# Constant matmuls in TensorE's waits around a selective scan and at the ends of attention, and an earlier load of the first expert weights

## What is computed

```
x = x + 0.5 * ffn(ln(x))     # gated, four 512-wide layers, ternary weights
x = x + mamba(ln(x))         # in_proj, conv of 4, x_proj, softplus, scan, out_proj
x = x + 0.5 * ffn(ln(x))     # the same weights again
x = x + 0.5 * moe(ln(x))     # 64 experts of 88, top 8 in 4 of 8 groups, 2 shared
x = x + attention(ln(x))     # 8 query heads, one key/value head, causal, 512 tokens
x = x + 0.5 * moe(ln(x))     # the same weights again
```

## Time and profile before

| | |
|---|---|
| median of three runs | 1762.87 us |
| the profiled execution | 1760.58 us, of which span 1758.8 us |
| TensorE busy | 1605.8 us (91%) |
| VectorE busy | 1272.3 us (72%) |
| ScalarE busy | 1016.4 us (58%) |
| GpSimd busy | 992.7 us (56%) |
| mean granted TensorE clock | 0.974 of 2.4 GHz |

### The profile page before, as it was taken

How to read it: one execution, slowest core, us unless ns; L and a number is a source line. 1 busy time by engine, 2 the same in 40 slices (tenths; PEclk the granted TensorE clock), 3 DMA queues, 4 the chain that set the end, 5 groups by cost and what they waited for, 6 DMA issues and landing times.

```text
span 1758.8 us, 24391 instructions
## 1 busy us (share of the span) xinstructions
PE 1605.8 (91%) x6936; PEld 1196.0 (68%) x6936; DVE 1272.3 (72%) x2156; ACT 1016.4 (58%) x2065; POOL 992.7 (56%) x955
## 2 busy tenths in 40 slices
PE   7997667877799989999899899998998999999998
PEld 5775323333367767777688677886886778878887
DVE  5555699999855756788578567885775678856665
ACT  4343655454434446676477666664776666656665
POOL 1101067766510028888433378894333888978887
PEclk9999789999999999999999999999999999999999
DMA  2000000000000036666300056663000566656674
GB/s 104 10 1 1 0 1 1 0 0 0 8 0 1 1 88 165 163 166 165 85 1 1 6 143 154 170 174 86 1 1 5 146 152 174 172 141 172 172 173 107
DMA packets 57678, 136.75 MB, mean 78 GB/s; under 512 B 10251, under 2 KB 33251, under 8 KB 57187
## 3 DMA queue, kind: packets, MB, share of 16 engines
q1 hardware_dynamic: 57571, 135.47, 30.0%
HBM read 133.33 MB, written 2.10 MB: 77 GB/s over the span
## 4 chain that ended last, share of the span: by engine, by line
PE 64%; DVE 4%; ACT 3%; issue 2%; POOL 2%; POOLq 0%; PEldq 0%; PEld 0%; DMA 0%; SPq 0%; DVEq 0%; ACTq 0%
PE ps L226 18%; PE ps L227 18%; PE ps L228 17%; PE ps L1488 2%; PE ps L1473 1%; PE ps L1474 1%; PE ps L1475 1%; PE ps L774 1%; POOL m_hc L984 1%; POOL e_lo L234 1%; PE ps L366 1%; PE ps L1476 0%; DVE p L1661 0%; PE ps L377 0%; PE ps L254 0%
## 5 line engine op out<-in xcount | busy, mean ns | idle before, releaser
L234 POOL TENSOR_TENSOR e_lo<-e_h,e_hi 128x512 fp32r<-128x512 f32 (+1 forms) x368 | 476.4, 1295 | 131.1 <-ACT e_hi L231 120.7
L1140 ACT ACTIVATE e_s<-ps 128x512 f32<-128x512 f32 (+1 forms) x368 | 220.4, 599 | 271.5 <-PE ps L228 270.8
L1296 DVE TENSOR_TENSOR ps<-e_s,ps 128x512 f32<-128x512 f32 x352 | 244.7, 695 | 179.3 <-PE ps L228 145.1
L226 PE MATMUL ps<-xn_hi,eh 128*128 128x512 f32 x704 | 284.8, 405 | 10.3 <-ACT e_s L1140 7.4
L227 PE MATMUL ps<-xn_lo,eh 128*128 128x512 f32 x704 | 279.5, 397 | 0.0
L228 PE MATMUL ps<-xn_hi,el 128*128 128x512 f32 x704 | 278.8, 396 | 0.0
L1301 DVE TENSOR_TENSOR e_h<-ps,rwb 128x512 f32<-128x512 f32 x352 | 243.3, 691 | 16.2 <-DVE ps L1296 4.8
L984 POOL TENSOR_TENSOR m_hc<-m_h,m_c 128x512 f32<-128x512 f32 x128 | 172.5, 1348 | 125.3 <-DVE m_h L940 122.9
L234 POOL TENSOR_TENSOR el<-e_raw,eh 128x128 fp32r<-128x128 f32 (+1 forms) x352 | 221.8, 630 | 26.7 <-ACT eh L1129 26.7
L231 ACT ACTIVATE e_hi<-e_h 128x512 fp32r<-128x512 f32 (+1 forms) x368 | 229.3, 623 | 7.4 <-DVE e_h L1301 7.3
L774 PE MATMUL ps<-m_hc,const 128*128 128x512 f32 x256 | 149.5, 667 | 48.8 <-POOL m_hc L984 43.9
(11 more groups left out here) (232 smaller groups left out, 3293.5 us busy)
## 6 DMA issues: line engine op xcount, KB each, us to landing
e_raw<-in_experts SPq DMA_DIRECT2D x176, 192.0 KB, 3.9
rwb<-rw_rows SPq DMA_DIRECT2D x64, 352.0 KB
rwb<-rw_rows SPq DMA_DIRECT2D x80, 256.0 KB
rwb<-rw_rows SPq DMA_DIRECT2D x32, 320.0 KB
rwb<-rw_rows SPq DMA_DIRECT2D x48, 192.0 KB
rwb<-rw_rows SPq DMA_DIRECT2D x32, 224.0 KB
rwb<-rw_rows SPq DMA_DIRECT2D x32, 160.0 KB
rwb<-rw_rows SPq DMA_DIRECT2D x80, 64.0 KB
```

Of the source, the lines that this page charges most:

```text
L226: pe.matmul(out, w_hi, x_hi, start=start, stop=False, skip_group_check=True)
L234: return eng.tensor_tensor(lo, full, hi.bitcast(F32), ALU.subtract)
L1140: act.activation(e_s[0:rows_, buf, :], ps[0:rows_, 4, :], ACT.Silu).then_inc(S["silu"], 1)
L1296: dve.tensor_tensor(ps[:, bank, :], e_s[:, buf, :], ps[:, 5, :], ALU.mult).then_inc(S["gated"], 1)
```

## The change

Nine calls of `spin` are added to TensorE's list: 20 before the loop of the projections, 8 at the top of each of its three turns, 18 before the last `x_proj`, 8 after it, 12 ahead of the wait of the last output projection of the mixer, 6 at the end of the mixer; and, at the end of each of the two attention phases, 10 before the last `out_proj` and 6 after it. Counted as they run, that is 20 + 24 + 18 + 8 + 12 + 6 + 2 x 16 = 120 constant matmuls. On SyncE's queue the store of the routing rows moves behind the first four loads of `e_raw`.

```diff
             one_spread(pe, L, LAST)
+            spin(pe, 6, 20)
             pe.wait_ge(*M("dt_w", 2))
             pe.wait_ge(*L("xn_lo", NB))
             with pe.Fori(0, NB - 1) as i:
+                spin(pe, 6, 8)
                 in_proj(i + 1, bass.ds((i + 1) * T, T))
                 x_proj(i)
+            spin(pe, 6, 18)
             x_proj(NB - 1)
+            spin(pe, 6, 8)
...
             def finish(i, blk, q):
                 if q == 4:
+                    if isinstance(i, int):
+                        spin(pe, 0, 12)
                     after(pe, "x_new", i)
...
             for ch in range(SLOTS):
                 moe_weights(sp, S, ch)
+            if not before:
+                moe_store_rows(sp, R, half)
             sp.wait_ge(*R(f"rw_out{half}", 16))
...
                 if not last:
                     q_proj(i + 1, cut(i + 1), 1)
                     score(i + 1, 0)
+                else:
+                    spin(pe, 0, 10)
                 out_proj(i, HEADS - 1)
+                if last:
+                    spin(pe, 0, 6)
...
             moe_load_small(sp, R1)
-            moe_store_rows(sp, R1, 0)
             moe_load_first(sp, E1A, 0, R1, None)
...
             mix_pe(pe, LN[1])
+            spin(pe, 0, 6)
             end_phase(pe)
```

## The result

The changed kernel takes 1748.4 us (median of four runs, 1746.81 to 1750.39), with 1762.5 us for the kernel before on the same chip: a ratio of 0.9923, 95% interval 0.9905 to 0.9942, so 14.1 us are gone. Measured once more, on another chip, it took 1747.9 us (five runs), with 1762.8 for the kernel before: ratio 0.9915 (0.9901 to 0.9928), 15.0 us less. The prediction was 1747, range 1741 to 1756. Both intervals lie more than the 0.3% away from no change that the prediction named as the bound of what can be told.

What follows compares the result with a forecast made beforehand. TensorE, mostly busy at full clock, was taken to lose time where waits let its clock fall. Terms -4.2 - 3.7 - 5.4 - 1.5 - 0.45 = -15.3 us gave 1745.3, or 1747.6 on the median; 1747 was taken, range 1741 to 1756.

Steps and rivals of the forecast that it cites:

- Projections: Projections of phase 1: spins fill TensorE's waits and hold the clock, -4.2 us, bounds -2 and -5.
- The gap of 2 us: Projections, before in_proj(1): 2.0 us left empty by the spins; if the clock falls there, only -2 us is gained.
- the signs that the prediction named: Profile after: clock 1.00 from 168 to 209, `bc` at 205.5 instead of 209.78, the scan's first product 4 us sooner.
- Mixer's end and layernorm: End of mixer and layernorm of phase 2: +0.3 hold-up, -4.0 from full clock, -3.7 us; bounds -2 and -5.7.
- Phase 3: Start of phase 3: earlier `e_raw` load saves 3.7 us of wait, full clock another 1.7; -5.4 us, bounds -3.7 and -6.
- First attention's end: First attention's end and phase 5's first tiles: -1.6 from full clock, +0.1 hold-up; -1.5 us, bounds -0.7 and -2.2.
- Second: Second attention's end: +0.75 as spins delay the next phase, -1.2 on its tiles; -0.45 us, bounds +0.7 and -1.2.
- C: Whole kernel: spins do not hold the clock, only the earlier load's gain remains; -3.6 us, 1759; chance 0.05.
- D: Ends of mixer and attention, last x_proj: spins at 0.42 to 0.45 us outlast their waits; +12 us, 1775; chance 0.03.
- B: Whole kernel: the clock holds at some places only; -9.4 us, 1753.5; chance 0.18.
- A: Four low-clock stretches: removed low time gives half of itself everywhere, 18 us, with the load 21.7; 1741; chance 0.06.

Runs made afterwards that it cites:

- spins_only: The changed kernel with the store of the routing rows put back ahead of the first expert-weight loads, all 120 spins kept: 1755.0 us, ratio 0.9949.
- the doubled kernel: The changed kernel with 36, 24 and 20 spins where it has 18, 12 and 10, so that they outlast their waits: 1756.1 us, ratio 0.9956.

## Why the prediction was right

Predicted were 1747 us and 15.3 us less; measured 1748.4 and 14.1, and 1747.9 and 15.0. The forecast is the case that happened. Its five parts, against the profile:

1. Projections: -4.2 predicted, -3.15 in the changed kernel's first profile, -4.1 in its second and in five others. The mechanism holds: in the second profile x_proj(3) stands 1.87 us nearer to the phase's first mean (2.0 predicted, passed through a loop in which VectorE is the bound), and `bc` comes 3.01 us behind it instead of 5.23, 2.2 less. The microsecond that the first profile is short of this went in the spread, ahead of the first spin, where the clock fell (2.08 us instead of 1.12). Three of the four profiles without spins in the projections have the fall at this place too (spreads of 1.20, 1.50 and 1.95 us), so spins are not needed for it. The gap of 2 us, in which the prediction let the clock fall for its lower bound, had a fall behind it in two of nine profiles, at a price of 1.5 us. Of the signs that the prediction named, three fell short by about that microsecond: `bc` was expected at 205.5 and came at 206.84, the first scan stands 2.9 us sooner instead of 4, and the clock from 168 to 175 us is 0.94 instead of 1.00. In the second profile `x_proj(3)` stands 43.37 us behind the phase's first mean instead of 44.33. Over the profiles of the table the spins are worth 65.7 - 61.3 = 4.4 us.
2. Mixer's end and layernorm: -3.7 predicted (+0.3 and -4.0), -3.5 measured (+0.14 and -3.64), alone 3.5. The 4.0 was a choice between 2 and 6, for the reason that other engines would end last in part; the gate's 1.07 us wait for GpSimd shows that they do. But the length of the low time before was taken as a fact of the kernel, and it is one draw: without spins the stage may be anything between 13.8 and 16.6.
3. Phase 3: -5.4 predicted, -5.38 measured, -5.35 with the load alone, and -5.3 in its time. Both terms hold (3.7 of wait, 1.7 of clock). This is the largest part and the cheapest: one call moved in a queue. The weighting behind it was not late, as the stage from the fourth product to phase 4 shows (207.41 before, 207.46 after).
4. First attention's end: -1.5 predicted, -1.50 measured.
5. Second: -0.45 predicted, -0.43 measured.

The five parts sum to -14.0 in the profile, with a start 0.2 later; of the rest, -1.44 at the start of the first attention and +1.44 on the way to phase 6 cancel. The text allowed 1.5 us either way for falls that come and go in places that the change does not touch, and both numbers are such falls. Behind ScalarE's `e_s`, which stands behind table loads for the routing scores, TensorE waits 1.88 us in both kernels. Before:

```profile
1070.57 0.50 PE L226 MATMUL ps<-xn_hi,eh 128*128 128x512 f32 x1 [1.88 <-ACT e_s L1140]
1070.91 0.40 PE L227 MATMUL ps<-xn_lo,eh 128*128 128x512 f32 x1
```

After:

```profile
1055.74 0.50 PE L226 MATMUL ps<-xn_hi,eh 128*128 128x512 f32 x1 [1.88 <-ACT e_s L1146]
...
1057.15 0.63 PE L227 MATMUL ps<-xn_lo,eh 128*128 128x512 f32 x1
```

The same wait, to the hundredth, is followed by a fall in one and by none in the other. The fall is in seven of the fourteen profiles: six of the eight of the changed kernel and its variants, and one of the six others. So the start of the first attention is luck by the repeated profiles, and of the 1.44 us on the way to phase 6 it stays open whether they are luck or a cost of the change.

The difference of a microsecond between forecast and median is within what the falls do, and is not explained further.

**The rivals.** C (spins do not hold the clock) would have left spins_only at or above before: it is 8.5 us below. D's mechanism is real where the spins outlast a wait, as the doubled kernel shows with its 8 us, but its condition, 0.42 us a spin, did not arise: the ten spins at the first attention's end take 2.45 us. B names what did happen in single executions (a fall in the gap, a slow spread), for 1.5 and 1.0 us where its lower bound of part 1 took 2.2. A would have given 1741. A mean clock of 0.974 is 0.052 x 1758.8 = 91 us at 1.2 GHz, one of 0.987 is 0.026 x 1745.0 = 45; half of the 46 that are gone would be 23 us. The span lost 13.8, of which 3.7 is the DMA wait; with the 1.0 us that the spins behind the projections hold up the next phases (0.14, 0.07 and 0.75) some 11 came from the clock. By the rule of the Trainium skill (TensorE: Matmul & The Clock Gate, section Terms: throttled time times one half) it would be those 23; the trace does not agree, by a factor of two, since VectorE is the bound in much of the low time that was removed: the loop of the projections has no idle time of VectorE in the earlier trace rows.

**What the six spins were for.** The prediction booked their cost (0.75 in the second end, 0.1 net in the first) and never asked whether the ten ahead of them would do alone. They do. This was the one question that the profile of before could have raised and the prediction left out: the earlier trace rows show the wait behind the projection as 0.82 us, and the earlier trace rows falls behind 2.79 us and more only. The six at the mixer's end and the eight behind the last `x_proj` were not left out by themselves in any run, so what they bring is not shown.

## What to carry to other kernels

Look first for a wait that should not be there: the late load cost 3.7 us of waiting and 1.7 us of the slower clock behind it, and moving one call removed both. Constant matmuls are worth having only in a wait that stays, with work behind it for which TensorE is the bound; size them so that they end before the wait does, for each 0.22 us over is paid in full, and read the wait from a profile in which the work ahead of it is fast already: it was 5.81 us and not 4.52 before the last projection here. Before a stage's length is booked as a gain or a loss, take the profile of the same program twice: here single stages of an unchanged program differ by 1.5 us through where the clock falls, and one by over 2 us for another cause.

## What had not been expected of the hardware

- The clock does not always fall at the same wait. A wait of 1.88 us was followed by a fall in seven of fourteen profiles, one of 1.29 us in seven of eleven; the wait of 2.98 us at the mixer's end by one in all four kernels without spins there, but the slow time lay on the projection, behind it, or over the whole layernorm, and cost from 0.7 to 3.5 us.
- A row of spins takes 0.223 us for each and 0.17 once (14 in 3.29 us, 36 in 8.20).
- Two multiplications or subtractions of 128 x 512 on VectorE and one on GpSimd that starts 0.3 us behind the first of them do not run side by side at full speed, and which engine pays can differ between executions of one program: 1.27 and 2.10 us, or 2.33 and 1.49. On a path that VectorE bounds this made 2.3 us.
- A row of spins that fills a wait on TensorE moved the work behind it by nothing that can be seen as long as it ended before the wait did: 0.84, 0.55, 0.41 and 0.31 us of remaining idle time were all enough.
